# Projections of a transformer layer in three products of fp16 halves, with fillers in equal shares and the norms' maximum behind the last low half

## What is computed

```python
def _L0_attn_ref(x, Wq, bq, Wk, bk, Wv, bv, Wo, bo):      # x: 16 x 1024 x 256, float32
    q = _split_heads(x @ Wq.T + bq)                       # 16 heads of 16
    k = _split_heads(x @ Wk.T + bk)
    v = _split_heads(x @ Wv.T + bv)
    scores = jnp.einsum('hbnd,hbmd->hbnm', k, q) * SCALE  # SCALE = 1/16
    attn = jax.nn.softmax(scores, axis=-1)
    out = jnp.einsum('hbnm,hbmd->hbnd', attn, v)
    return out @ Wo.T + bo
...
x = _layernorm(x + _L0_attn_ref(x, ...), axis=-1)
x = _layernorm(x + _L0_ffn_ref(x, ...), axis=-1)          # silu(x Wg) * (x Wu), then Wd: 256 -> 768 -> 256, int weights
```

## Time and profile before

| | us |
|---|---|
| median of three runs | 2694.0 |
| lowest, highest | 2688.95, 2698.48 |
| the profiled execution | 2687.43 |
| its span | 2685.4 |
| mean granted TensorE clock in it | 0.993 of 2.4 GHz |

### The profile page before, as it was taken

One profiled execution on the slowest core, in us unless ns is written; L12 is line 12 of the kernel. 1 busy time (PEld: TensorE's weight loads), 2 busy tenths in 40 slices (PEclk: granted clock), 3 DMA queues, 4 the chain that ended last, 5 costly groups with the idle time before them and its releaser, 6 DMA issues. The chain is left out here.

```text
span 2685.4 us, 47000 instructions
## 1 busy us (share of the span) xinstructions
PE 2585.0 (96%) x17294; PEld 934.6 (35%) x17294; DVE 1299.3 (48%) x2812; ACT 2131.6 (79%) x2370; POOL 539.7 (20%) x542
## 2 busy tenths in 40 slices
PE   6879999999999999999999999999999999999997
PEld 2223343333424333343433324333243433323334
DVE  4324545454554545545454554545545454553537
ACT  2887878788887888878788787888878788787881
POOL 2101211121221212211121221212211121221113
PEclk9999999999999999999999999999999999999998
DMA  4111121020202102121020202102121020201000
GB/s 155 49 54 48 33 77 41 29 88 25 88 29 79 50 15 94 33 77 41 29 88 25 88 30 77 52 14 95 34 76 41 29 88 25 88 30 56 26 15 34
DMA packets 81742, 144.08 MB, mean 54 GB/s; under 512 B 27584, under 2 KB 29504, under 8 KB 79424
## 3 DMA queue, kind: packets, MB, share of 16 engines
q1 hardware_dynamic: 79968, 139.81, 16.6%
q10 hardware_dynamic: 1504, 0.66, 0.1%
HBM read 88.48 MB, written 50.33 MB: 52 GB/s over the span
## 5 line engine op out<-in xcount | busy, mean ns | idle before, releaser
L603 ACT ACTIVATE probs<-psum 128x1024 f32<-128x1024 f32 x2048 | 1983.6, 1023 | 460.2 <-PE psum L1014 460.0
L1014 PE MATMUL psum<-probs,v 128*32 128x512 f32 x8192 | 989.6, 601 | 23.6 <-DVE flipped L854 20.9
L1014 PE MATMUL psum<-kstack,qstack 51*128 51x512 f16 x4096 | 629.8, 382 | 34.0 <-ACT probs L603 28.6
L1014 PEld LDWEIGHTS psum<-probs,v 128*32 128x32 f32 x8192 | 215.2, 109 | 534.5 <-issue 499.8
L1014 PEld LDWEIGHTS psum<-kstack,qstack 51*128 51x128 f16 x4096 | 134.0, 93 | 714.9 <-ACT probs L603 648.0
L512 POOL TENSOR_TENSOR ffn<-h,ffn 128x512 f16<-128x512 f32 x192 | 221.4, 1155 | 596.4 <-DVE ffn L773 496.9
L728 DVE SCALAR_TENSOR_TENSOR tanh_out<-tanh_out,psum 128x512 f32<-128x512 f32 x192 | 131.3, 684 | 289.8 <-ACT tanh_out L584 289.8
L505 POOL TENSOR_TENSOR rstd<-vareps,minus_half 128x2 f32<-128x2 f32 x128 | 89.7, 701 | 806.4 <-DVE vareps L792 806.4
L719 DVE SCALAR_TENSOR_TENSOR parts<-psum,scales,parts 128x512 f16<-128x512 f32 x128 | 95.3, 744 | 243.5 <-ACT parts L575 243.4
L491 POOL TENSOR_TENSOR squares<-parts 128x512 bf16<-128x512 f16 x128 | 132.3, 1042 | 349.9 <-DVE parts L719 241.4
L1014 PE MATMUL psum<-ffn,gateT 128*128 128x512 f16 x768 | 199.8, 383 | 0.3 <-DVE ffn L761 0.3
(11 more groups left out here) (102 smaller groups left out, 1543.8 us busy)
## 6 DMA issues: line engine op xcount, KB each, us to landing
parts_dram<-parts SPq DMA_DIRECT2D x64, 512.0 KB, 2.8
qstack<-parts_dram SPq DMA_DIRECT2D x384, 64.0 KB, 2.1
kstack<-parts_dram SPq DMA_DIRECT2D x384, 64.0 KB, 2.1
x_pre<-in_x_t SPq DMA_DIRECT2D x17, 1024.0 KB, 7.2
x_res<-in_L_attn_x SPq DMA_DIRECT2D x16, 1024.0 KB, 4.8
out<-x_res SPq DMA_DIRECT2D x32, 512.0 KB, 2.7
kstack<-shift_parts SPq DMA_DIRECT2D x384, 4.0 KB, 1.7
ffn<-in_L_ffn_w_gate SPq DMA_DIRECT2D x1, 768.0 KB, 9.6
```

Of the source, the lines that this page charges most:

```text
L603: nc.scalar.activation(probs[:, (STEPS * b + k) % SLOTS, 2 * pr:2 * pr + 2, :], scores[pr], ACT.Exp, scale=score_scale[par]).then_inc(prob ...
L1014: return nc.tensor.matmul(o, lhsT, rhs, start=start, stop=stop)
```

## The change

`Wq`, `Wk`, `Wv` and `Wo` are multiplied by a scale from the largest sum of absolute values (`w_scale`) and split into a high and a low fp16 half, once, ahead of batch 0 (`convert_projection`); the fp32 weights lie in `probs`, slot 0, until then. x and the attention's output are split the same way for each batch (`x16`, `out16`). A projection is then three fp16 products for each fp32 one: high by high, high by low, low by high (`TERMS`). An item of `qk` is 6 matmuls of 512 columns, one of `v` or `out` 12 of 256. The scales are undone in the drain of `out` and in `find_scale`. `evenly` divides the first twenty and the last twenty steps' fillers into equal shares and cuts items where a share ends. `reduce_norms`, `decide`, the reload of the flag and the last `prepare_shift` move to later steps. `reduce_xmax` moves up. The loads of the feed-forward weights stand behind the first `x_scaled`.

```diff
-COST = {"x1T": (4, 109), "qk": (2, 868), "norm": (1, 330), "v": (4, 434), "out": (4, 434),
+COST = {"x1T": (4, 109), "qk": (6, 216), "norm": (1, 330), "v": (12, 108), "out": (12, 108),
         "gate": (4, 216), "up": (4, 216), "down": (24, 108)}
+FULL_BLOCKS = (evenly(some("qk", 0, 1, 2, 3) + some("out", 0, 1, 2, 3)
+                      + [item for j in range(4) for item in some("x1T", j) + some("qk", 4 + j)], 20)
+               + [some("norm", *{3: (0,), 5: (1,)}.get(g, ())) + gate_up(g) for g in range(2 * HCHUNKS)]
+               + evenly(some("v", 0, 1) + some("down", 0) + some("v", 2, 3) + some("down", 1, 2, 3), 20))
-POOL_XMAX, POOL_NORMS = 16.2, 36.3
-DECIDE, RELOAD = 44, 50
+POOL_XMAX, POOL_NORMS = 12.2, 48.9
+DECIDE, RELOAD = 57, 58
-INTS, WMAX, WIDE = 24, 28, 56
+INTS, WMAX, WIDE = 24, 28, 58
-PREPARES = [PER_GROUP * g + PREPARE for g in range(GROUPS)]
+PREPARES = [PER_GROUP * g + PREPARE for g in range(GROUPS - 1)] + [STEPS - 4]
...
+            def convert_projection(tile, to, w):
+                nc.vector.tensor_scalar(to[:, 0, :, :], tile, w_scale[:, w:w + 1], None, ALU.mult)
+                dve.drain()
+                nc.vector.scalar_tensor_tensor(out=to[:, 1, :, :], in0=tile, scalar=w_scale[:, w:w + 1],
+                                               in1=to[:, 0, :, :], op0=ALU.mult, op1=ALU.subtract).then_inc(w16_ready, 1)
...
             def scale_x(hf, scale):
 
                 cols = slice(hf * HALF, (hf + 1) * HALF)
-                nc.vector.tensor_scalar(xT[:, :, cols], x_pre[:, :, cols], scale[:, S:S + 1], None, ALU.mult
-                                        ).then_inc(x_scaled, 1)
+                nc.vector.tensor_scalar(x16[:, 0, :, cols], x_pre[:, :, cols], scale[:, X_SCALE:X_SCALE + 1], None, ALU.mult)
+                dve.drain()
+                nc.vector.scalar_tensor_tensor(out=x16[:, 1, :, cols], in0=x_pre[:, :, cols],
+                                               scalar=scale[:, X_SCALE:X_SCALE + 1], in1=x16[:, 0, :, cols],
+                                               op0=ALU.mult, op1=ALU.subtract).then_inc(x_scaled, 1)
...
                 if odd:
                     dve.drain()
-                    nc.vector.transpose(outT[:, c, hf * HALF:(hf + 1) * HALF], scaled[:, hf, :]).then_inc(out_ready, 1)
+                    cols = slice(hf * HALF, (hf + 1) * HALF)
+                    nc.vector.transpose(flipped[:, hf, :], scaled[:, hf, :])
+                    dve.drain()
+                    nc.vector.tensor_copy(out16[:, 0, c, cols], flipped[:, hf, :])
+                    dve.drain()
+                    nc.vector.tensor_tensor(out16[:, 1, c, cols], flipped[:, hf, :], out16[:, 0, c, cols], ALU.subtract
+                                            ).then_inc(out_ready, 1)
...
                 elif kind == "qk":
...
-                    for k in range(lo, hi):
-                        ins = mm(o, w[:, k, c * P:(c + 1) * P], xT[:, k, hf * HALF:(hf + 1) * HALF],
-                                 k == 0, k == CHUNKS - 1)
+                    for m in range(lo, hi):
+                        k, (wp, xp) = m // 3, TERMS[m % 3]
+                        ins = mm(o, w[:, wp, k, c * P:(c + 1) * P], x16[:, xp, k, hf * HALF:(hf + 1) * HALF],
+                                 m == 0, m == count - 1)
```

More of the change, by code:

```diff
@@ L38 @@
 SCORE_BOUND = 70.0
-V_BOUND = 2.0 ** 16
+W_TOP = 2.0 ** 9
+BIAS_FLOOR = 2.0 ** -10
+TERMS = ((0, 0), (0, 1), (1, 0))
 NORM_MARGIN = 1.02
@@ L81, in gate_up, with evenly @@
     return [(kind, g) for g in gs for kind in ("gate", "up")]
-FULL_BLOCKS = ([some("qk", j) for j in range(4)] + [some("out", j) for j in range(4)]
-               + [some("x1T", j) + some("qk", 4 + j) for j in range(4)]
+def evenly(items, steps):
+    total = sum(COST[kind][0] * COST[kind][1] for kind, _ in items)
+    blocks = [[] for _ in range(steps // 2)]
+    at = 0
+    for kind, j in items:
+        count, cost = COST[kind]
+        where = [min(steps // 2 - 1, (at + cost * i + cost // 2) * (steps // 2) // total) for i in range(count)]
+        at += count * cost
+        for m in sorted(set(where)):
+            blocks[m].append((kind, j, where.index(m), count - where[::-1].index(m)))
+    return blocks
+FULL_BLOCKS = (evenly(some("qk", 0, 1, 2, 3) + some("out", 0, 1, 2, 3)
+                      + [item for j in range(4) for item in some("x1T", j) + some("qk", 4 + j)], 20)
                + [some("norm", *{3: (0,), 5: (1,)}.get(g, ())) + gate_up(g) for g in range(2 * HCHUNKS)]
-               + [some("v", 0), some("v", 1), some("down", 0), some("v", 2), some("v", 3),
-                  some("down", 1), some("down", 2), some("down", 3)])
-FULL = [item for block in FULL_BLOCKS for item in block]
+               + evenly(some("v", 0, 1) + some("down", 0) + some("v", 2, 3) + some("down", 1, 2, 3), 20))
+FULL = list(dict.fromkeys((kind, j) for block in FULL_BLOCKS for kind, j, *_ in block))
 def halves(kind, j):
@@ L280, in build @@
         ints = ffn[:, 0:3 * 1536]
+        WqT, WkT, WvT, WoT = [probs[:, 0, w, :].rearrange("p (c n) -> p c n", c=CHUNKS) for w in range(4)]
         ffn16 = ffn[:, :].bitcast(F16)
@@ L1069, in do_item @@
                 elif kind == "v":
[L1070 removed]
+                    each = count // 2
+                    for m in range(lo, hi):
+                        i, k, (xp, wp) = m // each, m % each // 3, TERMS[m % 3]
                         t = 2 * j + i
[L1072 to L1073 removed]
+                        ins = mm(o[:, i * DIM:(i + 1) * DIM], x16[:, xp, k, t * P:(t + 1) * P], Wv16[:, wp, k, :],
+                                 m % each == 0, m % each == each - 1)
                 elif kind == "out":
```

126 lines of the change are left out of this document (65 added, 61 removed).

## The result

The changed kernel takes 2600.4 us (median of 4 runs, 2597.9 to 2601.7) against 2693.2 for the kernel before in the same session: a ratio of 0.9656, with a 95% interval of 0.9638 to 0.9673, so 3.4% faster. The forecast was 2594 us, in a range of 2562 to 2625. The profiled execution took 2599.4 us with a span of 2597.3; before it was 2687.4 and 2685.4.

The account below looks back on a forecast made before the run. PE, 96% busy, was taken to bound the kernel, with a floor of 4.60 us for each pair of steps. 2687.4 - 112 - 22.7 + 31.6 - 1 + 4 = 2587.3, times 1.0025 gives 2594 us; range 2562 to 2625.

Parts of the forecast that it names:

- products, 14 batches: Projections in full batches: sixteen fp32 items each become fp16 products, 8.0 us a batch won, 112 us in fourteen.
- wait for `flipped`: PE's wait in full batches behind POOL's maximum of the norms: goes in all fourteen, 20.9 + 1.8 = 22.7 us won.
- wait for `flag`, 14 batches: PE's new wait ahead of the scores of step 58: 2.1 us a batch, 29.4 us lost in fourteen.
- falls of the clock behind it: PE at 1.2 GHz after the new flag wait: not in the forecast's sum; a rival with chance 0.10.
- batch 0: The flag wait in the first batch: some 2.2 us lost.
- start: Ahead of the first batch, longer DVE chain and weight loads ahead of the first store: +4 us, between -1 and +9.
- batch 15 and tail: Last batch: four `out` blocks go from 1.93 to 1.42 us, a pair from 4.86 to 4.60: -1.0 us.
- a pair lasts the longer of 4.60 and 2.93 + block: Two steps on PE: 2.93 us plus their block of filler products, never under the 4.60 us set by the exponentials.
- The slow rival: Projections' weight loads lie bare, 0.098 + 0.109 us a product: 2765 us, slower than before; chance 0.04.
- The choice of 0.16 us for the flag, and not 0.99: Flag's row on DVE takes its shortest time, POOL being idle; the rival of 0.99 gave 2606 us, chance 0.08.
- its rival: Each flag wait brings PE's clock down to 1.2 GHz: 15 x 1.9 = 28 us more, 2622 us; chance 0.10.

Follow-up runs that it names:

- moves_only: The kernel before (fp32 products, whole items) with only the moves of norms' maximum, flag's making and wait, and last shift; 2672.7 us, ratio 0.9955.
- whole_early: The changed kernel with whole items in place of equal shares, maximum of x at step 16.2 and flag made at step 54; 2605.5 us, ratio 0.9676.
- flag_early: The changed kernel with the flag made at step 54, before the sixth segment is taken, not at 57; 2566.7 us, ratio 0.9528.
- two_same_plan: The changed kernel, plan of blocks kept, with two products in place of three for each projection (less exact); 2582.8 us, ratio 0.9609.
- norms_back: The changed kernel with norms' maximum, flag's making and wait, and last shift back at their old steps, fp16 products and equal shares kept; 2601.2 us, ratio 0.9656.
- whole_items: The changed kernel with the old list of blocks (whole items outside the gates) in place of equal shares; 2782.0 us, ratio 1.0353.
- loads_late: The changed kernel with the three feed-forward weight loads issued behind the first load_shift, not ahead of the first store_parts; 2593.1 us, ratio 0.963.
- chain_longer: The changed kernel with the last subtraction of the output halves made twice, lengthening VectorE's chain before the flag; 2619.4 us, ratio 0.9745.
- two_terms: The changed kernel with two products in place of three for each projection (less exact), blocks planned anew; 2643.7 us, ratio 0.9839.
- whole_xmax: The changed kernel with whole items in place of equal shares and GpSimd's maximum of x put back to step 16.2; 2636.4 us, ratio 0.9791.
- reload_both: The changed kernel with late feed-forward weight loads, flag made at step 57 but waited for at step 60, not 58; 2559.9 us, ratio 0.951.
- both: The changed kernel with the flag made at step 54 and the feed-forward weight loads issued behind the first load_shift; 2560.8 us, ratio 0.9505.

## Why the prediction was right, point by point

Full batches at their steady distance: before 161.29, `moves_only` 160.07, `whole_early` 155.07, the changed kernel 153.95, `flag_early` 152.09. Against the terms of the prediction, in us (parts of the profiled span):

| term | forecast | measured | from |
|---|---|---|---|
| products, 14 batches | -112 | -106.1 | 14 x 7.58: 161.29 - 1.62 - 152.09 |
| wait for `flipped` | -22.7 | -22.7 | `moves_only`, 14 x 1.62 |
| wait for `flag`, 14 batches | +29.4 | +26.0 | `flag_early`, 14 x 1.86 |
| falls of the clock behind it | 0 | +4.7 | 3 x 1.55 |
| batch 0 | +2.2 | +6.0 | 155.91 for 149.91 |
| start | +4 | +5.0 | first scores at 58.82, before 53.80 |
| batch 15 and tail | -1.0 | -1.4 | 219.75 for 221.16 |
| sum | -100.1 | -88.5 | spans: 2597.3 - 2685.4 = -88.1 |

**Products.** The price of one product held (0.109), and so did the rule that a pair lasts the longer of 4.60 and 2.93 + block: `whole_early` and `two_same_plan` came within 0.3 us a batch of what it gives. The 7.58 split into 4.60 for fp16 in whole items (161.29 - 1.62 - 155.07) and 2.98 for the shares. The term was 0.4 us a batch too large. Most of that, 4 x 0.08, is in the four blocks of `x1T` with `qk`: I took 0.51 for each item, but such a block took 2.31 us before (893.67 to 895.98, the rows below are of the kernel before) and takes 1.88 now, 0.43 less.

```profile
893.67 0.66 PE L1017 MATMUL psum<-ident,x_res 128*128 128x128 f32 x4
...
895.98 0.61 PE L1014 MATMUL psum<-kstack,qstack 51*128 51x512 f16 x4
```

**The loads of weights.** The slow rival is out: 98 to 99 ns for each load of a projection's half, and none of it shows in a spacing of 109 ns.

```profile
L1046 PEld LDWEIGHTS psum<-Wv,x 128*128 128x128 f16 x768 | 71.8, 99 | 32.3 <-issue 23.8
```

The Trainium skill (TensorE: Matmul & The Clock Gate, Back-to-back issue gap) says that load and matmul both set the spacing, but pipelined, and not that they add; for a matmul by itself it has N / 2.4 + 2.5 ns, by which 256 columns would take 109 ns, an estimate. The trace of the changed kernel agrees with that estimate: 0.109 us, with a load for each product. The sum of both, 0.207 us, which the prediction took for the page's, is neither what the page says nor what the trace has.

**The wait that goes** went in all fourteen batches, as costed. The maximum of the norms blocks nobody in the new place: it starts at 788.61, and GpSimd's next work, at 804.67, has waited 9.46 us for VectorE.

```profile
788.61 0.19 POOL L502 TENSOR_TENSOR norm_safe<-norm,margin 128x2 f32<-128x2 f32 x1
794.84 0.37 POOL L504 PARTITION_ALL_REDUCE norm_all<-norm_safe  x1 [6.04 <-issue]
804.67 0.74 POOL L510 TENSOR_TENSOR rstd<-vareps,minus_half 128x2 f32<-128x2 f32 x1 [9.46 <-DVE vareps L815]
```

**The wait that comes** was 1.88 us where I had 2.1, by the very chain I had counted. The choice of 0.16 us for the flag, and not 0.99, was right: all sixteen take 0.158 to 0.160 us. By the Trainium skill (SBUF — State Buffer, SBUF: two separate sides) a VectorE instruction with two SBUF inputs and a GpSimd one exclude each other; the trace agrees, since GpSimd is idle at each of these rows. `norms_back` shows the other side: with the flag made beside the low halves again, its row is 0.99 us in all fourteen full batches.

**The clock** was the step that failed, in part. I left it at nothing and gave its rival 15 x 1.9. Neither is what came: the falls cost 4.7 us in the full batches, and in batch 0 three slow P (3.04, 3.61 and 3.14 us) take 4.0 us more than 1.92 each, so the term that I left at nothing was some 8.7 us, the largest part of the 11.6 by which the sum was off. It fell behind 3 of 14 rests in the full batches. In batch 0 the rest was 3.62 us, not some 2.2, as the step ahead of it has no block there and S(58) is due sooner; the P behind it took 3.61. What the prediction argued from, fourteen rests of 1.4 to 2.1 us without a fall, was true of the kernel before, but it said little about a rest of 2.1 us: thirteen of the fourteen were of 1.4 to 1.8 us, and one alone, of 2.13, was as long as the rest that I forecast. `norms_back` has five of 1.4 to 1.8 us without a fall and nine of 2.0 to 2.4 with 5.

**Luck.** A full batch was forecast at 153.9 us and took 153.95, but by errors of both signs: 0.4 us too much for the products, 0.2 too much for the flag's wait, 0.1 in the 161.4 that I started from. And the time itself is nearer than the sum: for the profiled execution I forecast 2587.3 us and it took 2599.4, 12 us more, while 2594 and 2600.4 are 6 apart. The factor of 1.0025 from the profiled execution to the median, 6.7 us, was in the kernel before and isn't in the changed one (2599.4 and 2600.4), so half of the error vanished by it.

**What stays open.** What decides whether a rest brings the clock down. The counts are of one profiled execution of each kernel, and of its fourteen full batches. The length has a part in it: no rest of 1.8 us or less was followed by a slow P there, and each of 7.1 to 8.1 us was (`whole_items`, 14 of 14). In between the length alone doesn't settle it: 0 of 1 at 2.1 us (before), 3 of 14 at 1.88 to 2.14 (the changed kernel, and again in `loads_late`), 8 of 14 at 1.88 to 2.14 (`two_same_plan`), 5 of 9 at 2.0 to 2.4 (`norms_back`), 9 of 14 at 2.64 or more (`chain_longer`), 10 of 14 at 2.1 to 2.4 and 11 of 14 at 2.7 to 3.0 (`two_terms`), and at 2.2 to 2.6 us 0 of 14 in `whole_xmax` and 6 of 14 in `whole_items`. Less work in the blocks around it goes with more falls in `two_same_plan`, but the last two kernels have the same blocks and the same rests for the flag and still differ. In `whole_items` the falls behind the flag come in every second batch, in the changed kernel in every fifth; so the moment at which a rest comes may count too, which no run here tests. Batch 0 is settled in part. Its time goes with the clock in it: `norms_back` takes 150.6 us with no slow P (granted clock 0.98 over the batch), `reload_both` 153.1 with 1.9 us of excess in P (0.97), the changed kernel 155.9 with 4.0 (0.96), `flag_early` 156.6 with 6.0 (0.94), in four slow P. But those of `flag_early` stand behind rests of 0.9 and 0.5 us for ScalarE, with no rest for the flag, and the kernel before has rests of these sizes in batch 0 and no slow P; what brings the clock down there is open.

**The version to keep.** `both` or `reload_both`: 0.9505 and 0.951 of the kernel before, 1.5 to 1.6% less than the changed kernel (0.9505 / 0.9656 = 0.984). As it was made, the move of the maximum was worth nothing (`norms_back` has the same time); with the flag made three steps sooner it is worth 1.3% (0.9656 to 0.9528).

## What to carry to other kernels

When a slow step is moved out of the way, what depends on it is queued anew, and the new place has a cost of its own: find the first point at which the result is ready (step 54 here) and put its use there, not behind the next long chain. Positions that were tuned together belong together: a share of work by cost moves every item when one cost changes, and two of my experiments, `whole_items` and `two_terms`, became slower by 7% and 2% than the kernel they came from, through a wait that the edit didn't name. A gain in work per block stops at the partner engine's floor, and spreading work so that all blocks lie just above that floor was worth 42 of the 106 us.

## What the runs showed of the hardware that I had not expected

- Rests of 1.9 us on a TensorE that is otherwise busy bring its clock from 2.4 to 1.2 GHz sometimes, 3 times in 14, and each fall costs 1.55 us: nearly as much again as the rest itself.
- A small reduction across partitions on GpSimd, with 0.37 us of work, holds the engine for 14 us; 6.2 us go by ahead of it and 7.2 behind it, in which the profile shows nothing that it waits for.
- Stores issued 4 us behind three loads of 0.8 MB each landed 4.9 us later than without them (40.84 against 35.97 us), though they were issued at the same time.
